# Projections and value products of two cross attentions put among the last batches, and normalised rows shared by VectorE and ScalarE

## The chip, the core and the metric

The program runs on one NeuronCore of a Trainium2 chip. The core has TensorE (PE: matmuls and transposes through an array of 128 x 128, with a separate load of the stationary operand, PEld), VectorE (DVE), ScalarE (ACT), GpSimd (POOL), and SyncE (SP), which only issues DMAs. Each engine works through its own queue in order and waits on semaphores for the others. Matmuls write to PSUM, eight banks of 512 float32 columns in 128 partitions. The metric is the device time of one execution in microseconds.

## What is computed

A Perceiver-like model of four layers on 32 sequences of 32 latent tokens with 256 features, in float32. Each layer has a cross attention to a context of 257 tokens a sequence, a self attention and a feed-forward part, most of them with mixtures of experts. The parts that the change touches most, cut down:

```python
# layer 1 cross attention (16 heads of 64, one key/value head), parallel feed-forward
h = layer_norm(x)                      # 1024 rows of 256
kv = layer_norm(context) @ Wkv
att = softmax(q(h) @ k.T) @ v          # by sequence
x = x + att @ Wo + (silu(gate) * up) @ Wff2
# layer 3 cross attention (8 heads of 64) over context and latents
x = x + (softmax(q @ keys.T) @ tokens) @ Wv @ Wout
# layer 0 experts
h = layer_norm(x); r = rms_norm(h); e = argmin(dist(r, centroids))
x = x + h + expert[e](r)
```

Every layer norm is a mean and a deviation by row, and then `(x - mean) / deviation`.

## The kernel before, in words

Twelve stages follow one another, one function each, with a barrier between them (`free_sems`, L87). X holds the 1024 rows as NT = 8 tiles of 128 rows. A stage normalises X into H, transposes H into HT and works on that.

**Norm** (L158). The last stage's end has already taken statistics tile by tile (`take`, L196: an addition to X, then L203 and L206 for its tiles). At the entry ScalarE takes the root (L235), VectorE the reciprocal (L213), and VectorE alone writes the eight normalised tiles one after the other (`rows`, L186), each with an increment of one semaphore. **Flip** (L238): TensorE transposes in the order half 0 chunk 0, half 0 chunk 1, half 1 chunk 0, half 1 chunk 1, four tiles each (L262), and waits before each for its tile. ScalarE copies the chunk 0 banks (L275, L279), VectorE the chunk 1 banks (L290, L294), which on VectorE is behind all eight rows. Eleven entries use this with a counter of rows; the twelfth, layer 0's experts, has a further norm (L2086).

**Layer 0's experts** (L2013). VectorE writes eight tiles of R (L2086), adds H to the whole of X in one instruction (L2088), and then makes its two copies of the transposed R (L290). TensorE's router (L1227, 16 products of 8 columns) needs these copies. From the router's result VectorE derives the places of all tokens (L2093 and on, `place_rows`, `place_weights`, `mark_columns`, `find_rows`, L756 to L841); GpSimd then gathers rows by indirect DMA (L997), and `ex.vector` begins with the first expert's units (L1168).

**Layer 1's cross attention** (L2110). After the query projection and the first feed-forward matrix, TensorE multiplies the second one tile by tile (L2293, banks 0 to 2 in turn) with keys and values of the first two batches in between; VectorE adds each tile to X (L2431). Then come 32 batches. In iteration b TensorE does `sim(b + 1)` (L2258, banks 0 to 3), `flip_probs(b)` (L2269, banks 4 and 5), `keys_values(b + 3)` (L2241, bank 6), `weigh(b)` (L2283, bank 7) and `flip_values(b + 3)` (L2247). ScalarE does the exponentials (L2342) and copies, `copy_out(b)` (L2355) writing 32 columns of AT; VectorE the maxima (L2410), reciprocals (L2415) and copies; GpSimd multiplies by the reciprocals (L2190). AT shares its memory with the hidden units of the feed-forward. The output projection (L2315) waits for all 32 batches, does 8 tiles of 8 matmuls with two tiles to a bank, and VectorE adds pairs of tiles to X and takes their statistics (L2456). Four filler matmuls (`keep_busy`, L81) end TensorE's part.

**Layer 3's cross attention** (L3300). 32 batches likewise, `flip_probs(b)` (L3409, L3412), `sim(b + 2)`, `weigh(b)` (L3425, L3428); the results replace QW. Behind the last one TensorE waits for ScalarE's copy (L3514) and makes 8 value products (L3459), for four pairs of heads by two halves of the sequences, alternately in banks 0 (copied by ScalarE, L3534) and 1 (by VectorE, L3592). When all are copied, the projection follows (L3466), added by pairs (L3596). The memory of OT is that of hat, tokens and probs of the batches.

## Time and profile before

| | |
|---|---|
| median of 3 runs | 1978.56 us (1977.77 to 1979.53) |
| profiled execution | 1979.34 us, span from first to last instruction 1977.6 us |
| TensorE matmul busy | 1811.5 us, 92% |
| VectorE busy | 1075.2 us, 54% |
| ScalarE busy | 808.4 us, 41% |
| GpSimd busy | 564.9 us, 29% |
| mean granted TensorE clock | 0.963 of 2.4 GHz |
| stage of layer 1's cross attention | 391.3 to 703.4 us |
| stage of layer 3's cross attention | 1520.2 to 1765.1 us |

Times within the trace count from the first instruction. A row of the timeline names an engine, a line of the kernel and an operation, and in brackets how long the engine had been idle before it and what ended that. A matmul in float32 leaves two records, and matmuls are pipelined, so their ends overlap; the weight loads show better when TensorE really went on. The granted clock is 1.00 at 2.4 GHz and 0.50 at 1.2 GHz.

### The profile page before, as it was taken

Reading aid. Unit: us, or ns where it says so; the run is one execution under the profiler, and the core shown is the slowest. Engines: PE = TensorE matmul, PEld = TensorE weight load, DVE = VectorE, ACT = ScalarE, POOL = GpSimd, SP = SyncE. Lnnn points to the kernel's source line nnn. Section 1 sums busy time; section 2 is a strip of 40 time slices with the busy share of each in tenths; the row PEclk is TensorE's granted clock in tenths of the full one; section 3 lists DMA queues with packets and bytes.
Section 4 is the critical chain, followed back from the end, with each engine's and each line's share of the span. In section 5 each row is a group of like instructions: output and inputs, shape, how many; then the busy total and the mean of one; then the engine's idle time right before and its main releaser. Section 6 shows DMA issues by size and latency. Waiting matters only on the chain. (4 is left out here: it accounts for less than half of the span.)

```text
span 1977.6 us, 43225 instructions
## 1 busy us (share of the span) xinstructions
PE 1811.5 (92%) x16810; PEld 1405.4 (71%) x16810; DVE 1075.2 (54%) x2695; ACT 808.4 (41%) x2340; POOL 564.9 (29%) x617
## 2 busy tenths in 40 slices
PE   8999779999999889799999989998588899987898
PEld 6886569844777756699999957776454477755787
DVE  7787841352366337875555545555665555437511
ACT  6663621122266334233333325553410566616232
POOL 4441313100144202311121113331311466515242
PEclk9999889999999999999999999998699999998899
DMA  4120068560233110041899641111011355300397
GB/s 146 55 56 5 3 239 296 192 217 30 57 102 100 28 54 3 8 195 58 310 330 334 225 169 50 50 45 54 2 54 57 89 157 155 102 1 2 109 338 253
DMA packets 87010, 233.92 MB, mean 118 GB/s; under 512 B 9776, under 2 KB 45136, under 8 KB 80304
## 3 DMA queue, kind: packets, MB, share of 16 engines
q1 hardware_dynamic: 78992, 213.90, 32.1%
q0 software_dynamic: 5664, 15.47, 2.5%
q8 instruction: 121, 1.98, 0.4%
q10 hardware_dynamic: 2176, 2.10, 0.3%
q14 instruction: 57, 0.47, 0.1%
HBM read 216.21 MB, written 12.07 MB: 115 GB/s over the span
## 5 line engine op out<-in xcount | busy, mean ns | idle before, releaser
L2190 POOL TENSOR_TENSOR l1x_probs<-l1x_probs,l1x_total 128x512 f32<-128x512 f32 x64 | 65.0, 1038 | 211.4 <-DVE l1x_total L2415 211.4
L1515 PE MATMUL PS<-weights,l0x_ctxT 128*128 128x256 f32 x512 | 121.0, 386 | 0.8 <-DVE l0x_kp L1803 0.7
L1048 PE MATMUL PS<-l1f_xT,l1f_slot 128*128 128x128 f32 x1024 | 117.0, 275 | 0.0
L1048 PEld LDWEIGHTS PS<-l1f_xT,l1f_slot 128*128 128x128 f32 x1024 | 115.7, 192 | 0.1
L1515 PEld LDWEIGHTS PS<-weights,l0x_ctxT 128*128 128x128 f32 x512 | 94.0, 190 | 15.9 <-issue 3.5
L2923 POOL TENSOR_TENSOR l2x_probs<-l2x_probs,l2x_total 128x512 f32<-128x512 f32 x64 | 65.1, 1038 | 136.3 <-DVE l2x_total L3097 136.3
L81 PE MATMUL PS<-consts 128*128 128x256 f32 x340 | 85.1, 403 | 17.5 <-PEq L87 15.8
L81 PEld LDWEIGHTS PS<-consts 128*128 128x128 f32 x340 | 67.5, 203 | 31.6 <-issue 19.5
L235 ACT ACTIVATE std<-moments,eps 128x8 f32<-128x8 f32 x13 | 3.9, 301 | 203.1 <-DVEq L173 133.7
L1175 DVE SCALAR_TENSOR_TENSOR l1f_product<-PS,l1f_slot,l1f_side 128x128 f32<-128x128 f32 x128 | 36.0, 344 | 65.9 <-ACT l1f_side L1131 50.9
L3401 PE MATMUL PS<-l3x_keysT,l3x_QW 128*128 128x289 f32 x256 | 67.7, 407 | 1.7 <-issue 1.7
L1002 POOL DMA_INDIRECT l1f_out_dram<-l1f_out,l1f_sort_target_row x23 | 22.6, 985 | 159.5 <-DVE l1f_out L1158 159.5
L1131 ACT ACTIVATE l1f_side<-PS,l1f_slot 128x128 f32<-128x128 f32 x128 | 36.5, 368 | 66.0 <-PE PS L1048 62.9
L3425 PE MATMUL PS<-tagged,l3x_QT 128*128 128x256 f32 x256 | 60.6, 379 | 1.9 <-ACT tagged L3510 1.9
L2950 PE MATMUL PS<-l2x_ctxT,weights 128*128 128x257 f32 x256 | 61.1, 381 | 1.0 <-DMA l2x_ctxT<-in_ctxT_dram 1.0
L1048 PE MATMUL PS<-HT,weights 128*128 128x128 f32 x512 | 60.7, 280 | 0.9 <-DVE l1f_gated L1180 0.7
L1048 PEld LDWEIGHTS PS<-HT,weights 128*128 128x128 f32 x512 | 60.1, 197 | 1.8 <-DVE l1f_gated L1180 1.1
L1695 ACT ACTIVATE l0x_sq<-PS 128x256 f32<-128x256 f32 x128 | 47.8, 385 | 32.6 <-PE PS L1515 32.6
L1175 DVE SCALAR_TENSOR_TENSOR l1f_product<-PS,weights,l1f_side 128x128 f32<-128x128 f32 x120 | 33.8, 344 | 49.7 <-ACT l1f_side L1131 41.0
L2958 PE MATMUL PS<-weights,l2x_ctxT 128*128 128x256 f32 x256 | 60.4, 379 | 0.0
L3043 ACT ACTIVATE l2x_probs<-PS,l2x_top 128x257 f32<-128x257 f32 x128 | 59.2, 482 | 1.3 <-DVE l2x_top L3091 1.3
L2232 PE MATMUL PS<-HT,weights 128*128 128x512 f32 x128 | 57.3, 608 | 2.2 <-DVE l1x_AT L2379 2.2
(659 smaller groups left out, 4648.5 us busy)
## 6 DMA issues: line engine op xcount, KB each, us to landing
l1f_slot<-in_experts_up_dram SPq DMA_DIRECT2D x16, 2056.0 KB
weights<-in_experts_up_dram SPq DMA_DIRECT2D x8, 2056.0 KB, 7.8
weights<-in_experts_down_dram SPq DMA_DIRECT2D x21, 640.0 KB, 4.3
weights<-in_experts_up_dram SPq DMA_DIRECT2D x10, 1024.0 KB
l1f_slot<-in_experts_down_dram SPq DMA_DIRECT2D x16, 640.0 KB, 4.1
l0x_ctxT<-in_ctxT_dram SPq DMA_DIRECT2D x32, 257.0 KB, 2.6
l1x_ctxT<-in_ctxT_dram SPq DMA_DIRECT2D x32, 257.0 KB
l2x_ctxT<-in_ctxT_dram SPq DMA_DIRECT2D x32, 257.0 KB, 2.6
```

Source lines behind the costliest of these rows:

```text
L81: self.nc.tensor.matmul(self.PS[:, bank, 0:2 * P], self.ident, self.consts[:, 0:2 * P], start=True, stop=True)
L1048: done = nc.tensor.matmul(PS[:, bank + a, m * P:(m + 1) * P], mat[:, c, m * P:(m + 1) * P], x, start=(c == 0), stop=(c == 1))
L1175: done = nc.vector.scalar_tensor_tensor(p[:, m, :], PS[:, 2 * u + 1, m * P:(m + 1) * P], w["b3"][:, 4 * u + m:4 * u + m + 1], self.side[u] ...
L1515: last = nc.tensor.matmul(PS[:, 2 * (b % 2) + k, half * D:(half + 1) * D], ctxT[b % SLOTS][:, c, half * P:(half + 1) * P], kw[:, c, k * D: ...
L2190: nc.gpsimd.tensor_tensor(p, p, bcast(total[b % 2][:, 2 * n:2 * n + 2], 2, KEYS), ALU.mult).then_inc(probs_done, 1)
L2232: done = nc.tensor.matmul(PS[:, 2 * (n % 2) + g, :], ff1[:, c, (g * HB + m) * P:(g * HB + m + 1) * P], core.HT[:, c, half * 512:(half + 1) ...
L2923: nc.gpsimd.tensor_tensor(p, p, bcast(total[b % 2][:, 2 * n:2 * n + 2], 2, 2 * P), ALU.mult).then_inc(probs_done, 1)
L2950: last = nc.tensor.matmul(PS[:, 4 + 2 * o, 0:CTX], wk[:, c, o * P:(o + 1) * P], ctxT[b % 2][:, c, :], start=(c == 0), stop=(c == 1))
L2958: last = nc.tensor.matmul(PS[:, 5, half * D:(half + 1) * D], ctxT[b % 2][:, c, half * P:(half + 1) * P], wv[:, c, :], start=(c == 0), stop ...
L3043: done = nc.scalar.activation(probs[b % 2][:, u, :], PS[:, u, 0:CTX], ACT.Exp, bias=top[b % 2][:, u:u + 1], scale=-1.0, accum_out=total[b ...
L3401: done = nc.tensor.matmul(PS[:, 2 * (b % 2) + u, 0:KEYS], QW[:, c, b, 4 * u:4 * u + 4, :].rearrange("p h q -> p (h q)"), keysT[b % 2][:, c ...
L3425: nc.tensor.matmul(PS[:, 6 + c, 0:2 * P], tokens[b % 2][:, half, c * P:(c + 1) * P], probsT[b % 2][:, half, :], start=(half == 0), stop=False)
```

## The change

1. **Norm rows.** At eleven entries VectorE first computes shift = -mean / deviation (one instruction for all tiles), then writes tiles 0, 2, 4, 6, 7; ScalarE, after the root, waits for the shift and writes tiles 1, 3, 5 as `scale * x + shift`. Two counters take the place of one, and all who waited (transposes, GpSimd, SyncE's stores of rows) wait for the two.
2. **Layer 0's experts.** The addition of H to X moves from before VectorE's copies to behind `find_rows`.
3. **Layer 1's cross attention.** Tile 7 of the feed-forward product (bank 7) goes behind `sim(0)`, its addition behind the first reciprocals; `weigh(0)` waits for it. Tile 0 of the projection goes before `weigh(30)`, tile 1 before `weigh(31)`; each tile waits for its own four batches. The last two tiles have banks of their own and are added one by one.
4. **Layer 3's cross attention.** The value products go by halves: products 0 to 3 for the first 16 sequences (all copied by ScalarE), 4 to 7 for the others (by VectorE); product 0 goes before the last `weigh`. The projection of the first four tiles waits for ScalarE's copies only. The last two tiles are added one by one.

The core of the diff; the same two-counter form and the call of `scalar_rows` come at all eleven entries:

```diff
+ROWS_BY_DVE, ROWS_BY_ACT = (0, 2, 4, 6, 7), (1, 3, 5)
...
+        self.shifts_dve += 1
+        nc.vector.scalar_tensor_tensor(c.shift[:], c.moments[:, :, 0], -1.0, c.rstd[:], ALU.mult, ALU.mult).then_inc(self.shift_done, 1)
+        for t in ROWS_BY_DVE:
             nc.vector.tensor_scalar(dst[:, t, :], src[:, t, :], c.moments[:, t, 0:1], c.rstd[:, t:t + 1],
-                                    ALU.subtract, ALU.mult).then_inc(rows_done, 1)
+                                    ALU.subtract, ALU.mult).then_inc(dve_done, 1)
+    def scalar_rows(self, act, src, dst, rows_done):
+        c, nc = self.core, self.core.nc
+        _, act_done = rows_done
+        self.shifts_act += 1
+        act.wait_ge(self.shift_done, self.shifts_act)
+        for t in ROWS_BY_ACT:
+            nc.scalar.activation(dst[:, t, :], src[:, t, :], ACT.Identity, bias=c.shift[:, t:t + 1], scale=c.rstd[:, t:t + 1]).then_inc(act_done, 1)
+    def wait_rows(self, eng, rows_done):
+        dve_done, act_done = rows_done
+        eng.wait_ge(dve_done, len(ROWS_BY_DVE))
+        eng.wait_ge(act_done, len(ROWS_BY_ACT))
     def statistics(self, dve):
...
+                    if isinstance(rows_done, tuple):
+                        if t in ROWS_BY_ACT:
+                            pe.wait_ge(rows_done[1], ROWS_BY_ACT.index(t) + 1)
+                        else:
+                            pe.wait_ge(rows_done[0], ROWS_BY_DVE.index(t) + 1)
+                    else:
+                        pe.wait_ge(rows_done, t + 1)
                     to, rows = c.PS[:, 2 * half + ch, (t % 4) * P:(t % 4 + 1) * P], src[:, t, ch * P:(ch + 1) * P]
...
+            norm.scalar_rows(act, core.X, core.H, rows_done)
...
-            dve_step(dve, nc.vector.tensor_tensor(core.X[:], core.X[:], core.H[:], ALU.add))
             flip.vector(dve, XT)
...
             ex.places.find_rows(dve)
+            dve_step(dve, nc.vector.tensor_tensor(core.X[:], core.X[:], core.H[:], ALU.add))
             ex.vector(dve)
...
+        def ff_bank(t):
+            return t % 3 if t < NT - 1 else 7
+        def out_bank(t):
+            return (6, 6, 5, 5, 4, 4, 1, 2)[t]
...
                     pe.wait_ge(out_copied, b)
+                else:
+                    pe.wait_ge(ff_added, NT)
...
             pe.wait_ge(less_v_done, 1)
-            for t in range(NT):
+            def feed_forward(t):
+                for m in range(HB):
+                    done = nc.tensor.matmul(PS[:, ff_bank(t), 0:D], hidden[:, m, t * P:(t + 1) * P], ff2[:, m, :], start=(m == 0), stop=(m == HB - 1))
+                done.then_inc(ff_done, 1)
+            def project(t):
+                pe.wait_ge(out_copied, TB * t + TB)
+                for m in range(HB):
+                    done = nc.tensor.matmul(PS[:, out_bank(t), (t % 2) * D:(t % 2 + 1) * D], AT[:, m, t * P:(t + 1) * P],
+                                            wo[:, m, :], start=(m == 0), stop=(m == HB - 1))
+                done.then_inc(out_done, 1)
+            for t in range(NT - 1):
                 if t >= 3:
                     pe.wait_ge(ff_added, t - 2)
-                for m in range(HB):
-                    done = nc.tensor.matmul(PS[:, t % 3, 0:D], hidden[:, m, t * P:(t + 1) * P], ff2[:, m, :], start=(m == 0), stop=(m == HB - 1))
-                done.then_inc(ff_done, 1)
+                feed_forward(t)
                 if t in (0, 4):
                     keys_values(t // 4)
                 elif t in (2, 6):
                     flip_values(t // 4)
-            pe.wait_ge(ff_added, NT)
+            pe.wait_ge(ff_added, NT - 1)
             sim(0)
+            feed_forward(NT - 1)
             keys_values(2)
             flip_values(2)
             for b in range(B):
...
                 flip_probs(b)
                 if b + 3 < B:
                     keys_values(b + 3)
+                if b == B - 2:
+                    pe.wait_ge(v_copied, B)
+                    project(0)
+                elif b == B - 1:
+                    project(1)
                 weigh(b)
                 if b + 3 < B:
                     flip_values(b + 3)
-            pe.wait_ge(out_copied, B)
-            for t in range(NT):
-                for m in range(HB):
-                    done = nc.tensor.matmul(PS[:, 4 + t // 2, (t % 2) * D:(t % 2 + 1) * D], AT[:, m, t * P:(t + 1) * P],
-                                            wo[:, m, :], start=(m == 0), stop=(m == HB - 1))
...
-                nc.vector.tensor_tensor(core.X[:, t, :], PS[:, t % 3, 0:D], core.X[:, t, :], ALU.add).then_inc(ff_added, 1)
+                nc.vector.tensor_tensor(core.X[:, t, :], PS[:, ff_bank(t), 0:D], core.X[:, t, :], ALU.add).then_inc(ff_added, 1)
+            def add_out(tiles):
+                first, n = tiles[0], len(tiles)
+                dve.wait_ge(out_done, tiles[-1] + 1)
+                x = core.X[:, first:first + n, :]
+                at = (first % 2) * D
+                written = nc.vector.tensor_tensor(x, PS[:, out_bank(first), at:at + n * D].rearrange("p (t d) -> p t d", t=n), x, ALU.add)
+                norm.take(dve, written, tiles)
+            for t in range(NT - 1):
+                add_feed_forward(t)
                 if t in (1, 5):
                     scale_keys_values(t // 4)
-                elif t in (3, 7):
+                elif t in (3, 6):
                     copy_values(t // 4)
             tops(0)
-            scale_keys_values(2)
             for n in range(2):
                 weights(0, n)
+            add_feed_forward(NT - 1)
+            scale_keys_values(2)
             copy_values(2)
             for b in range(B):
                 if b + 1 < B:
...
                     weights(b + 1, 1)
                 if b + 3 < B:
                     copy_values(b + 3)
-            for n in range(NT // 2):
-                dve.wait_ge(out_done, n + 1)
-                x = core.X[:, 2 * n:2 * n + 2, :]
-                written = nc.vector.tensor_tensor(x, PS[:, 4 + n, :].rearrange("p (t d) -> p t d", t=2), x, ALU.add)
-                norm.take(dve, written, (2 * n, 2 * n + 1))
+            for tiles in ((0, 1), (2, 3), (4, 5), (6,), (7,)):
+                add_out(tiles)
         cn.loads = B // cn.SLOTS
...
+        def out_bank(t):
+            return 4 + t // 2 if t < NT - 1 else 2
...
-            for b in range(B):
-                flip_probs(b)
-                if b + 2 < B:
-                    sim(b + 2)
-                weigh(b)
-            pe.wait_ge(px_copied, B)
-
-            for n in range(2 * M):
-                m, half = n // 2, n % 2
+            def values(n):
+                half, m = divmod(n, M)
+                pe.wait_ge(px_copied, (half + 1) * (B // 2))
                 if n >= 2:
-                    pe.wait_ge((out_act, out_dve)[n % 2], n // 2)
+                    pe.wait_ge(*((out_act, n - 1) if n - 2 < M else (out_dve, n - 1 - M)))
                 for par in range(2):
                     for c in range(C):
                         at = (2 * m + par) * DH
                         done = nc.tensor.matmul(PS[DH * par:DH * (par + 1), n % 2, :], wv[:, c, at:at + DH], QW[:, c, half * (B // 2):(half + 1) * (B // 2), 2 * m + par, :],
                                                 start=(c == 0), stop=(c == 1))
                 done.then_inc(out_done, 1)
-            pe.wait_ge(out_act, M)
-            pe.wait_ge(out_dve, M)
+            for b in range(B):
+                flip_probs(b)
+                if b + 2 < B:
+                    sim(b + 2)
+                if b == B - 1:
+                    values(0)
+                weigh(b)
+            for n in range(1, 2 * M):
+                values(n)
             for t in range(NT):
+                if t % 4 == 0:
+                    pe.wait_ge((out_act, out_dve)[t // 4], M)
                 for m in range(M):
-                    done = nc.tensor.matmul(PS[:, 4 + t // 2, (t % 2) * D:(t % 2 + 1) * D], OT[:, m, t * P:(t + 1) * P], wout[:, m, :],
+                    done = nc.tensor.matmul(PS[:, out_bank(t), (t % 2) * D:(t % 2 + 1) * D], OT[:, m, t * P:(t + 1) * P], wout[:, m, :],
                                             start=(m == 0), stop=(m == M - 1))
-                if t % 2:
-                    done.then_inc(proj_done, 1)
+                done.then_inc(proj_done, 1)
             core.keep_busy(0, 4)
...
                 copy_px(b)
-            for n in range(0, 2 * M, 2):
-                act.wait_ge(out_done, n + 1)
-                nc.scalar.activation(OT[:, n // 2, 0:512], PS[:, 0, :], ACT.Identity, bias=v_bias[:, n // 2:n // 2 + 1]).then_inc(out_act, 1)
+            for m in range(M):
+                act.wait_ge(out_done, m + 1)
+                nc.scalar.activation(OT[:, m, 0:512], PS[:, m % 2, :], ACT.Identity, bias=v_bias[:, m:m + 1]).then_inc(out_act, 1)
...
             dve.wait_ge(v_bias_copied, 1)
-            for n in range(1, 2 * M, 2):
-                dve.wait_ge(out_done, n + 1)
-                nc.vector.tensor_scalar(OT[:, n // 2, 512:1024], PS[:, 1, :], v_bias[:, n // 2:n // 2 + 1], None, ALU.add).then_inc(out_dve, 1)
-            for n in range(NT // 2):
-                dve.wait_ge(proj_done, n + 1)
-                x = core.X[:, 2 * n:2 * n + 2, :]
-                written = nc.vector.tensor_tensor(x, PS[:, 4 + n, :].rearrange("p (t d) -> p t d", t=2), x, ALU.add)
-                norm.take(dve, written, (2 * n, 2 * n + 1))
+            for m in range(M):
+                dve.wait_ge(out_done, M + m + 1)
+                nc.vector.tensor_scalar(OT[:, m, 512:1024], PS[:, m % 2, :], v_bias[:, m:m + 1], None, ALU.add).then_inc(out_dve, 1)
+            for tiles in ((0, 1), (2, 3), (4, 5), (6,), (7,)):
+                first, n = tiles[0], len(tiles)
+                dve.wait_ge(proj_done, tiles[-1] + 1)
+                x = core.X[:, first:first + n, :]
+                at = (first % 2) * D
+                written = nc.vector.tensor_tensor(x, PS[:, out_bank(first), at:at + n * D].rearrange("p (t d) -> p t d", t=n), x, ALU.add)
+                norm.take(dve, written, tiles)
         @block.gpsimd
```

## Rows read from the trace of the kernel before

**Rows 1.** Timeline (start, busy us), weight loads, last batches of layer 1.
```profile
666.63 0.88 PEld L2283 LDWEIGHTS PS<-l1x_probsT,l1x_V 128*64 128x64 f32 x16 [1.20 <-issue]
668.43 0.42 PEld L2269 LDWEIGHTS PS<-consts,l1x_probs 128*128 128x128 f32 x4 [0.92 <-issue]
669.37 0.42 PEld L2269 LDWEIGHTS PS<-consts,l1x_probs 128*128 128x128 f32 x4 [0.52 <-POOL l1x_probs L2190]
671.07 0.88 PEld L2283 LDWEIGHTS PS<-l1x_probsT,l1x_V 128*64 128x64 f32 x16 [1.28 <-issue]
672.75 1.38 PEld L2315 LDWEIGHTS PS<-weights,l1x_AT 128*128 128x128 f32 x7 [0.81 <-ACT l1x_AT L2355]
```

**Rows 2.** One line, layer 1's projection: ns min/median/max, first to last start.
```profile
L2315 PE MATMUL PS<-weights,l1x_AT x128: 379/379/483, 672.8 to 700.3; 128*128 128x256 f32 x128
```

**Rows 3.** Timeline, all engines, from layer 1's feed-forward into its batches.
```profile
521.63 0.18 PEld L2258 LDWEIGHTS PS<-l1x_kvT,l1x_QT 64*128 64x128 f32 x1 [0.92 <-DVE X L2431]
522.70 0.73 PEld L2241 LDWEIGHTS PS<-l1x_ctxT,l1x_centred_kv 128*128 128x128 f32 x4 [0.33 <-issue]
526.42 0.17 DVE L2415 RECIPROCAL l1x_total<-l1x_total 128x2 f32<-128x2 f32 x1 [0.75 <-ACT l1x_probs L2342]
526.50 0.18 PEld L2258 LDWEIGHTS PS<-l1x_kvT,l1x_QT 64*128 64x128 f32 x1 [1.94 <-issue]
```

**Rows 4.** Timeline, weight loads, end of layer 3's cross attention.
```profile
1730.09 1.59 PEld L3425 LDWEIGHTS PS<-tagged,l3x_QT 128*128 128x128 f32 x8 [1.14 <-ACT tagged L3506]
1733.40 0.20 PEld L3459 LDWEIGHTS PS<-l3x_QW,weights 128*64 128x64 f32 x4 [1.09 <-ACT l3x_QW L3514]
1748.31 0.73 PEld L3466 LDWEIGHTS PS<-weights,l3x_QT 128*128 128x128 f32 x4 [1.79 <-issue]
```

**Rows 5.** One line, the value products of layer 3.
```profile
L3459 PE MATMUL PS<-l3x_QW,weights x64: 592/592/643, 1733.4 to 1746.8; 128*64 128x512 f32 x64
```

**Rows 6.** Timeline, ends of layer 1's cross attention and of layer 2's experts.
```profile
700.49 1.89 PE L81 MATMUL PS<-consts 128*128 128x256 f32 x8
700.69 0.69 DVE L2456 TENSOR_TENSOR X<-PS,X 128x512 f32<-128x512 f32 x1 [5.15 <-PE PS L2315]
702.20 0.25 DVE L206 BATCH_NORM_AGGREGATE moments<-stats 128x2 f32<-128x6 f32 x2
703.37 0.34 SPq L126 DMA_DIRECT2D weights<-in_pack_dram  x1
...
1520.26 1.10 PE L81 MATMUL PS<-consts 128*128 128x256 f32 x4 [0.70 <-PEq L87]
```

**Rows 7.** Timeline, entry of layer 1's experts.
```profile
838.85 2.71 DVE L186 TENSOR_SCALAR tagged<-X,moments,rstd 128x256 f32<-128x256 f32 x8
841.61 0.53 PEld L262 LDWEIGHTS PS<-consts,tagged 128*128 128x128 f32 x5 [0.18 <-DVE tagged L186]
```

**Rows 8.** One line, ScalarE, 128x256 with bias and scale, layer 3.
```profile
L3488 ACT ACTIVATE l3x_QT<-l3x_ctx,ctx_shift,ctx_rstd x64: 587/600/626, 1562.8 to 1720.8; 128x256 f32<-128x256 f32 x64
```

**Rows 9.** Timeline, entry of layer 2's cross attention.
```profile
1156.71 2.50 PEld L262 LDWEIGHTS PS<-consts,tagged 128*128 128x128 f32 x13 [0.19 <-DVE tagged L186]
```

**Rows 10.** Timeline, layer 0's experts, up to the first expert.
```profile
260.91 2.28 DVE L2088 TENSOR_TENSOR X<-X,tagged 128x2048 f32<-128x2048 f32 x1
264.07 5.19 PE L1227 MATMUL PS<-l0f_centm,l0f_XT 128*128 128x8 f32 x32 [1.91 <-DVE l0f_XT L290]
283.09 1.20 POOL L997 DMA_INDIRECT l0f_rows_in<-l0f_rows_dram,l0f_sort_token_row  x1 [26.83 <-DVE l0f_sort_token_row L836]
298.94 0.69 DVE L1168 TENSOR_TENSOR l0f_hidden<-PS,l0f_side 128x512 f32<-128x512 f32 x1 [16.10 <-ACT l0f_side L1119]
```

**Rows 11.** Windows: length, PE PEld DVE ACT POOL busy, clock, DMA, GB/s.
```profile
264.00:266.00 2.00, 1.93 (x18) 1.96 (x18) 0.52 (x1) 1.20 (x7) 0.00 (x0) 1.00 1.24 378
266.00:269.40 3.40, 3.26 (x16) 3.16 (x16) 0.03 (x1) 0.00 (x0) 0.00 (x0) 0.50 0.56 193
...
842.30:846.00 3.70, 3.70 (x34) 3.70 (x34) 0.69 (x1) 1.55 (x2) 3.47 (x4) 1.00 0.94 318
```

98 lines of the change are left out of this document (64 added, 34 removed).

## The prediction

> **What bounds the kernel now.** I read three views in this order. First the page: TensorE is busy for 92% of the span, so what can still be won lies in the gaps between its instructions, not in less work; the change removes no matmul. Then, for each place that the diff touches, the timeline in narrow stretches, TensorE's weight loads above all: a load that starts late with a releaser in brackets is a gap, and its size stands there. Last the windows with the granted clock, for the places where a gap is followed by slow matmuls. The change goes at five kinds of them: the end of layer 1's batch loop [rows 1, 2], the step from its feed-forward into the batches [rows 3], the end of layer 3's loop [rows 4, 5], the last additions of both stages [rows 6], and in front of transposes the entries of stages [rows 7 to 9] and the router of layer 0's experts, which waits for a large addition [rows 10, 11].
>
> **Layer 1, last batches.** Before weigh(30), both halves of flip_probs(31), weigh(31) and the first projection matmul the loads sit idle for 1.20, 0.92, 0.52, 1.28 and 0.81 us: 4.73 in all [rows 1]. The projection is 64 matmuls, 128 records, the first at 672.8, the last at 700.3 [rows 2]: 0.215 us a record, 3.44 us a tile of 16. The change puts tile 0 before weigh(30) and tile 1 before weigh(31), and each later tile waits for its own four batches only, so all but tile 7 are free to go. Both inserts (3.44) are longer than the gaps that they fill (1.20, 1.28), and while they run the next inputs arrive: by the times of before GpSimd's shares for batch 31 land at 669.3 [rows 1], and flips(30) (ends 1.20 before 666.63, 665.4) plus tile 0 (3.44) plus weigh(30) (0.88) is 669.7. What is queued behind weigh(30) is ScalarE's copy_out(30) and then copy_probs(31); it comes after flips(31), which are later too, so it is no new wait. What is left of the five gaps is pipeline drain. Bounds: 4.73, and 3.9, if each junction keeps a drain of 0.16 (a record takes 0.379, the next starts 0.215 after it [rows 2]). I take 4.3, the middle.
>
> **Layer 1, feed-forward.** Before sim(0) the loads are idle 0.92, before sim(1) 1.94 [rows 3]. Now tile 7 (3.44) goes between sim(0) and keys_values(2). Call S the start of sim(0). Before, sim(1) is at S + 4.87. After, S comes 3.44 + 0.05 earlier (it waits for the addition of tile 6, about as near as that of tile 7 was), sim(0) takes 1.07, tile 7 3.44, and keys_values(2) to sim(1) goes as before without the 1.94: 526.50 - 1.94 - 522.70 = 1.86 [rows 3]. That is S - 3.49 + 6.37 = S + 2.88, 2.0 earlier. The exponentials, at S + 4.79 by the second reciprocal [rows 3], are done before S + 6.37, and VectorE's addition of tile 7 fits between that reciprocal and scale_keys_values(2), 1.4 us. weigh(0) gets a new wait for that addition, which by then is over a microsecond old. The batch loop behind has its own pace and starts 2.0 earlier.
>
> **Layer 3.** The gaps of the loads are 1.14 (before the last weigh), 1.09 (before the value products) and 1.79 (before the projection): 4.02 [rows 4]. Value product 0 goes into the first, products 1 to 3 no longer wait for the last copy, and the projection of the first four tiles needs ScalarE's copies only, which are long done. A product's records have 512 columns and run on after their loads: the last starts at 1746.8 and takes 0.592 [rows 5], so that only 0.9 of the last gap is empty for certain. Bounds 4.02, and 2.7 (0.98 and 0.93 after a drain of 0.16 each, less 0.1, and 0.9). I take 3.0, nearer the low one.
>
> **The single last tiles.** At the end of layer 1's cross attention VectorE's last pair goes from its addition (0.69, at 700.69) to the end of its aggregates at 702.45, and the next stage starts at 703.37 [rows 6]. With one tile these 1.76 are about 1.1 (half of each instruction, some fixed part kept). But TensorE's four filler matmuls end at 702.38, and where they held the barrier (into layer 3's cross attention) the next stage's first matmul came 0.70 after them, its first other instruction a little sooner [rows 6]. So the next stage can't start before 703.05: 0.3 gained, not 0.65. Bounds 0 and 0.6. Twice: 0.65.
>
> **Normalised rows on two engines.** Eleven norms change. At the entry of layer 1's experts eight rows on VectorE take 2.71 us, 0.33 apart; the last reaches TensorE at 841.61, and five transposes (0.53) follow [rows 7]. After: a small shift instruction goes ahead (some 0.08 of VectorE's time) and VectorE has five rows, so its last is there at about 840.7. ScalarE's three cost 0.60 each by the nearest row, the same form with two per-partition operands (I space them 0.50 apart, as VectorE's 0.41 are 0.33 apart) [rows 8]: ready at 839.65, 840.15, 840.65. Row 3 then comes no earlier than before (840.24), and from it on 13 transposes at 0.11 are the bound: 841.67 against 842.14. Gain 0.47, also for the router, which follows at once. That holds where transposes run at the upper clock level: layer 0 self, layer 1 self and experts, layer 3 self (first norm) and experts, five times: 2.35. In the other six the transposes take 0.2 each and form an unbroken row (13 loads in 2.50) [rows 9]; rows are not late there, and the shift and ScalarE's slower first row can cost some 0.05 each: -0.3. In layer 1 cross they wait for another matmul anyway. Together 2.05; from -1 (ScalarE's rows late by as much as they are now early) to 3.4 (0.65 five times).
>
> **Layer 0 experts.** X + H is 2.28 us in front of VectorE's two copies, and the router waits 1.91 for them, to 264.07 [rows 10]. It moves behind find_rows, where VectorE is idle for 16.1 us until 298.94 [rows 10]: cost nothing under that cover, 2.28 without it. The first copy then goes where the addition went, at 260.91, and the router starts where TensorE is free, at 264.07 - 1.91 = 262.16: 1.9 gained. The second part is clock. The router's first 18 matmuls ran at granted 1.00 (2.4 GHz), the next 16 at 0.50 (1.2 GHz) [rows 11]; before them TensorE had been nearly idle for 1.9 us. In layer 1 the router has no such gap and all 34 are at 1.00 [rows 11]; the fall comes behind it. So I expect 3.5 us instead of 5.19, 1.55 more: 3.45 together. What follows (sorting, gathers) hangs on the router by a chain and moves with it.
> The moved addition overlaps GpSimd's first gathers; the first takes 1.20 at 283.09 [rows 10], with small VectorE instructions beside it. The Trainium skill, SBUF — State Buffer, section Who interferes with whom, says that a VectorE instruction with two SBUF inputs takes a port pair from GpSimd and that the later of the two fully blocks; it infers, without showing, that descriptor generation is spared. By the blocking rule the sum would come to up to 1965.4, by the inference to 1963.1. No row here has such an overlap; I take 0, since the gather's 1.20 beside short VectorE instructions is no sign of a full block, and keep 2.28 as the other bound.
>
> **Sum.** 4.3 + 2.0 + 3.0 + 0.65 + 2.05 + 3.45 = 15.45. The profiled execution has a span of 1977.6 (1979.34 with what lies around it); the median of the three runs is 1978.56, 0.8 below that execution. 1978.56 - 15.45 = **1963.1**.
>
> **Rivals.**
> (a) ScalarE's rows win nothing, since row 3 or 5 comes later than reckoned: the 2.35 go, 1965.5. For: 0.60 a row against 0.41. Against: five rows of VectorE end 0.9 earlier whatever ScalarE does.
> (b) Layer 0's experts win little: the moved addition holds the gathers (2.28), or the clock falls in the router all the same (1.55). 1964.7 to 1965.4. The first is a port that GpSimd would have to wait for, its price the addition's length; the second has for it that the fall in layer 1 came right behind the router.
> (c) The inserts shift the last batches' waits instead of filling them, so that half of layer 1's and layer 3's ends stays: 3.65 less, 1966.8. Against: every input of the inserted work is four or more batches old.
> (d) It doesn't do what it says: what is won in a stage is lost in front of the next, on weights or a barrier. Only some 3 us remain, 1975.5. Against: stage entries wait for the barrier alone (released by L87, the barrier) [rows 6].
> (e) Slower: TensorE's clock falls in the packed projections. All 128 records of layer 1's are within 379 to 483 ns now [rows 2]; at the lower level they double. If its 27.5 us all run so, 1963.1 + 27.5 = 1990.6. It decides from 19.5 us of matmuls at 1.2 GHz on (15.5 to cancel the gain, 4 to be slower). Against: gaps are filled, and in the rows clocks fall behind gaps or narrow matmuls.
>
> **How the numbers follow.** Chances: forecast 0.57, (a) 0.12, (b) 0.14, (c) 0.09, (d) 0.04, (e) 0.04. All low bounds together give 3.9 + 2.0 + 2.7 + 0 - 1 - 0.4 = 7.2 (1971.4); all high ones 4.73 + 2.0 + 4.02 + 1.2 + 3.4 + 3.45 = 18.8 (1959.8). The range takes (a), (b), (c) and two of them at once: 1959.3 to 1969. 0.2% is 4.0 us, about what a measurement of this kernel can tell from no change: faster is the forecast with (a) to (c), 0.92; same is (d), 0.04; slower (e), 0.04.
>
> **What would show it.** In the profile after: loads of the projection at once behind flips(30) and flips(31); no gap over 0.4 us between weigh(31) and the end of the projection; sim(1) 2.0 earlier relative to the feed-forward; in layer 3 no gap between products and projection; the last row-bound transposes 0.5 earlier after the reciprocal; the router of layer 0 in about 3.5 us, 1.9 earlier; the first gather still at 1.2. I am wrong if the stage of layer 1 cross (391.3 to 703.4) shortens by less than 5 us or that of layer 3 (1520.2 to 1765.1) by less than 2.5, or if the gathers take 3 us.

## The result and the profile after

The changed kernel takes 1959.75 us in the median of eight runs (1957.67 to 1971.24), the kernel before 1978.56 in eight beside it (1973.59 to 1982.61): a ratio of 0.9916, 95% interval 0.9899 to 0.9933. Run once more later, without a line changed, it gave 1963.8 (0.9921, 0.9897 to 0.9945); all fourteen runs together have the median 1962.3. Forecast were 1963.1. The profiled execution spans 1957.4 us, the one before 1977.6.

The page of after: TensorE is busy for 1800.9 us, 10.6 less than before, although no matmul is gone, so part of the gain is the same work at a higher clock (mean granted 0.967, before 0.963).

```profile
span 1957.4 us, 43250 instructions
PE 1800.9 (92%) x16810; PEld 1399.4 (71%) x16810; DVE 1066.5 (54%) x2675; ACT 826.2 (42%) x2373; POOL 567.1 (29%) x617
PEclk9999889999999999999999989999699999997899
```

**Layer 1, last batches.** Timeline of the weight loads (start, busy us, then engine, line, operation; in brackets the idle time before and what ended it).

```profile
657.16 3.32 PEld L2341 LDWEIGHTS PS<-weights,l1x_AT 128*128 128x128 f32 x16
660.81 0.85 PEld L2327 LDWEIGHTS PS<-l1x_probsT,l1x_V 128*64 128x64 f32 x16 [0.33 <-issue]
661.84 0.86 PEld L2311 LDWEIGHTS PS<-consts,l1x_probs 128*128 128x128 f32 x8 [0.17 <-issue]
...
666.32 0.85 PEld L2327 LDWEIGHTS PS<-l1x_probsT,l1x_V 128*64 128x64 f32 x16 [0.33 <-issue]
667.34 8.71 PEld L2341 LDWEIGHTS PS<-weights,l1x_AT 128*128 128x128 f32 x41 [0.17 <-issue]
```

The five gaps of [rows 1], 4.73 us, are 0.33, 0.17, none, 0.33 and 0.17 now, which I read as the drain between one group of matmuls and the next. From the first load of sim(29) to the first filler it is 45.88 us before and 41.78 after; 4.10 won.

```profile
654.39 0.18 PEld L2258 LDWEIGHTS PS<-l1x_kvT,l1x_QT 64*128 64x128 f32 x1 [0.17 <-issue]
700.27 1.70 PEld L81 LDWEIGHTS PS<-consts 128*128 128x128 f32 x8
```

```profile
646.17 0.18 PEld L2300 LDWEIGHTS PS<-l1x_kvT,l1x_QT 64*128 64x128 f32 x1 [0.17 <-issue]
687.95 1.70 PEld L83 LDWEIGHTS PS<-consts 128*128 128x128 f32 x8
```

**Layer 1, feed-forward.** The same view of after. Sim(0) starts 10.01 earlier than in [rows 3]. The first tile of the feed-forward already starts 6.34 earlier (484.70, before 491.04), so 3.67 are tile 7 and what was waited for; sim(1) comes 6.54 behind it instead of 4.87, and is 8.34 earlier: 2.00 won.

```profile
511.62 0.18 PEld L2300 LDWEIGHTS PS<-l1x_kvT,l1x_QT 64*128 64x128 f32 x1 [0.54 <-DVE X L2487]
512.69 3.32 PEld L2335 LDWEIGHTS PS<-weights,l1x_AT 128*128 128x128 f32 x16 [0.33 <-issue]
518.16 0.18 PEld L2300 LDWEIGHTS PS<-l1x_kvT,l1x_QT 64*128 64x128 f32 x1 [0.17 <-issue]
```

**Layer 3.** The gaps of [rows 4] were 1.14, 1.09 and 1.79; they are 0.81, 0.33 and 0.81.

```profile
1713.42 1.59 PEld L3504 LDWEIGHTS PS<-tagged,l3x_QT 128*128 128x128 f32 x8 [0.81 <-issue]
1715.98 0.20 PEld L3533 LDWEIGHTS PS<-l3x_QW,weights 128*64 128x64 f32 x4 [0.33 <-issue]
1728.20 1.81 PEld L3550 LDWEIGHTS PS<-weights,l3x_QT 128*128 128x128 f32 x9 [0.81 <-issue]
```

**The single last tiles.** All engines at the end of layer 1's cross attention. VectorE is done at 689.47, the fillers at 690.05, and the next stage's first matmul comes 0.96 after them, where one row of [rows 6] had made me expect 0.70. From the first filler load to the next stage's root on ScalarE it was 3.20 us before, and is 3.12: 0.08 won.

```profile
688.16 1.89 PE L83 MATMUL PS<-consts 128*128 128x256 f32 x8
688.37 0.42 DVE L2494 TENSOR_TENSOR X<-PS,X 128x256 f32<-128x256 f32 x1 [2.35 <-PE PS L2341]
689.29 0.18 DVE L230 BATCH_NORM_AGGREGATE moments<-stats 128x2 f32<-128x6 f32 x1
691.01 1.10 PE L83 MATMUL PS<-consts 128*128 128x256 f32 x4 [0.96 <-PEq L89]
691.07 0.30 ACT L259 ACTIVATE std<-moments,eps 128x8 f32<-128x8 f32 x1 [21.62 <-DVEq L176]
```

**Rows by two engines**, the entry of layer 1's experts. From VectorE's first instruction behind the reciprocal to the end of the transposes it is 2.86 us (824.51 to 827.37), before 3.29 (838.85 to 842.14 [rows 7]): 0.43 won. ScalarE's three rows take 1.59 together, 0.50 apart, and end with VectorE's five, at 826.4.

```profile
824.51 0.28 DVE L195 SCALAR_TENSOR_TENSOR shift<-moments,rstd 128x8 f32<-128x8 f32 x1
824.72 1.73 DVE L197 TENSOR_SCALAR tagged<-X,moments,rstd 128x256 f32<-128x256 f32 x5
824.83 1.59 ACT L206 ACTIVATE tagged<-X,shift,rstd 128x256 f32<-128x256 f32 x3 [0.59 <-DVE shift L195]
825.97 1.40 PEld L292 LDWEIGHTS PS<-consts,tagged 128*128 128x128 f32 x13 [0.29 <-ACT tagged L206]
```

**Layer 0's experts.** The router starts at once behind the matmuls ahead of it and its 32 loads take 3.65 us, all at 2.4 GHz. But the first gather takes 3.14 where [rows 10] had 1.20. It starts 0.22 after the moved addition and ends 1.07 after that has ended; the gathered rows are transposed 8.74 after it began, before 6.04.

```profile
261.56 3.65 PEld L1261 LDWEIGHTS PS<-l0f_centm,l0f_XT 128*128 128x128 f32 x32
278.91 2.29 DVE L2141 TENSOR_TENSOR X<-X,tagged 128x2048 f32<-128x2048 f32 x1
279.13 3.14 POOL L1031 DMA_INDIRECT l0f_rows_in<-l0f_rows_dram,l0f_sort_token_row  x1 [23.29 <-DVE l0f_sort_token_row L866]
287.87 0.29 PEld L1062 LDWEIGHTS PS<-consts,l0f_rows_in 128*128 128x128 f32 x2 [6.89 <-DMA l0f_rows_in<-l0f_rows_dram,l0f_sort_token_row]
```

Added up by places, these make less than the 20.2 us between the two spans. The rest lies where the diff changes nothing. Windows of after, then of before (length, busy of PE, PEld, DVE, ACT, POOL, granted clock, DMA, GB/s): the entry of layer 1's cross attention, where TensorE ran at 1.2 GHz for 4 us after, and before from 392 to 403.

```profile
388.00:392.00 4.00, 3.81 (x15) 3.19 (x16) 2.06 (x7) 2.06 (x5) 1.44 (x3) 0.57 0.59 174
392.00:396.00 4.00, 3.00 (x15) 1.87 (x15) 3.51 (x9) 1.38 (x2) 0.00 (x0) 1.00 0.30 102
```

```profile
392.00:396.00 4.00, 3.38 (x16) 3.01 (x16) 2.67 (x8) 0.78 (x1) 0.89 (x2) 0.54 0.80 263
396.00:403.00 7.00, 6.00 (x14) 3.28 (x13) 5.21 (x13) 1.35 (x2) 0.00 (x0) 0.53 0.29 88
```

By the table of stage lengths below, that stage is 3.0 us longer with 6.8 us of low time than with 3.4. Five more such stretches (at 737, 894, 1375, 1453 and 1771 before) are gone after, while one is new (1163 to 1171). Is that the change's doing or chance? And do the parts add up to the whole?

### The profile page after: what moved, and what is told of

Its sections match the earlier page's. It is cut to its first block and busy times, and to the rows that moved or that the text cites. A ratio compares the mean times of both kernels' runs of the same rounds, so it can differ in the third digit from the quotient of the medians.

```text
span 1957.4 us, 43250 instructions
## 1 busy us (share of the span) xinstructions
PE 1800.9 (92%) x16810; PEld 1399.4 (71%) x16810; DVE 1066.5 (54%) x2675; ACT 826.2 (42%) x2373; POOL 567.1 (29%) x617
```

## Experiments

Twelve more programs ran, two of them the kernels before and after once more. Theory A says that the low stretches of the clock fall where chance puts them, theory B that the change removes them, theory L that the addition holds the gather.

### Each part alone

`only_rows`, `only_l1x`, `only_l3x` and `only_move` are the kernel before with one part of the diff each. The last three also carry the second counter of the norm rows, but it stays unused: VectorE writes all eight rows, as before. Beyond that, the last one is only this:

```diff
-            dve_step(dve, nc.vector.tensor_tensor(core.X[:], core.X[:], core.H[:], ALU.add))
             flip.vector(dve, XT)
...
             ex.places.find_rows(dve)
+            dve_step(dve, nc.vector.tensor_tensor(core.X[:], core.X[:], core.H[:], ALU.add))
             ex.vector(dve)
```

> The kernel before with one part of the change alone: the normalised rows of eleven norms by VectorE (five) and ScalarE (three). The change as a whole won 18.8 us by the medians, but by a comparison of the two traces only some 13 of them (4.1 + 2.0 + 3.4 in the cross attentions, 3.5 in layer 0's experts) stand where the prediction put them; five short stretches in which the clock was at 1.2 GHz before (737 to 741, 894 to 898, 1375 to 1379, 1453 to 1458, 1771 to 1775) are gone, and one is new. Theory A (the clock's stretches move by accident when anything is shifted): this kernel gains its 2 us of rows (0.4 to 0.6 at each of five entries), and a clock sum that may go either way by up to 5: 1971 to 1979, with another set of low stretches than either kernel. Theory B (the denser transposes are what keeps the clock up at the entries): the stretches behind entries of layer 2 self, layer 2 experts and the second norm of layer 3 self are gone here as in the whole change, and the gain is 5 us or more.

> The kernel before with layer 1's cross attention changed alone (feed-forward tile 7 behind the first sim, projection tiles 0 and 1 among the last batches, single last tiles). Both theories: inside that stage the trace shows 2.0 us won by the first two sims, 4.1 to 4.3 at the last batches and 0.2 to 0.3 at the last tiles, 6.4 together. Theory A: the low stretches behind it (737 to 741, 894 to 898, entries of layers 2 and 3) are then another set than before, so the time is 1972 with an accident of up to 5 either way. Theory B: they stay where they were, since no transposes change: 1972, within 1.

> The kernel before with layer 3's cross attention changed alone. Both theories: nothing before 1730 us differs from before, and from there to the next stage's first instruction 3.0 to 3.4 us are won, 0.75 of it between the last weigh and the value products and 2.7 before the projection. Time 1975. Behind it theory A allows other low stretches in layer 3's self attention and experts (up to 2 either way); theory B none. It tells also how steady the pattern of low stretches ahead of the edit is between two executions: nothing there differs, so whatever moves there is the chip's.

> The kernel before with the addition of layer 0's experts moved behind the search for rows, alone. In the trace of the whole change the first gather took 3.14 us instead of 1.20 while the addition (2.29) ran, and the first gathered rows were transposed 8.7 us after that gather began, not 6.0. Theory L (the addition holds the gather, the prediction's rival b, its first half): the first gather takes 3.1 here too, starts 3.9 earlier than before, and of these 3.9 about 3.2 reach the first expert's matmuls. Theory D (the delay is the weights' transfers, which come earlier too): gather 1.2 to 1.5 here. The router's 34 matmuls start 1.9 earlier and take 3.6 in either. Time 1975 (theory L), with accidents of the clock up to 5 either way if theory A holds.

Measured in twelve runs each, beside 35 of before with the median 1978.28: rows 1977.14 (ratio 0.9990, 0.9978 to 1.0003), layer 1 1970.02 (0.9962, 0.9951 to 0.9973), layer 3 1977.26 (0.9999, 0.9987 to 1.0011), moved addition 1977.22 (0.9996, 0.9984 to 1.0008). The gains 1.1, 8.3, 1.0 and 1.1 make 11.5; the whole has 16 to 17. The traces are sharper than the times. The last batches of layer 1 win 4.09 in `only_l1x`, as in the whole. The last tiles win 0.08 there, where I had expected 0.2 to 0.3. `only_l3x` wins 2.54 in its stage, not 3.0 or more. In `only_move` the gather behaves as in the whole, which is what theory L says:

```profile
279.71 2.29 DVE L2129 TENSOR_TENSOR X<-X,tagged 128x2048 f32<-128x2048 f32 x1
279.92 3.15 POOL L1019 DMA_INDIRECT l0f_rows_in<-l0f_rows_dram,l0f_sort_token_row  x1 [24.05 <-DVE l0f_sort_token_row L855]
```

The gather began 3.17 us earlier than before, not 3.9, since the router's loads took 4.26 us here and not 3.6. Of that, 1.75 reached VectorE's first product of the first expert (297.19, before 298.94), not 3.2.

And `only_l3x`, which does the same as before for 1700 us, has a low stretch at 185 to 190 where the kernel before has none (first its window, then that of before):

```profile
185.00:190.00 5.00, 4.03 (x18) 3.14 (x17) 3.70 (x10) 1.17 (x2) 0.00 (x0) 0.66 0.10 31
```

```profile
185.00:190.00 5.00, 4.12 (x19) 2.44 (x20) 3.35 (x9) 1.17 (x2) 0.00 (x0) 1.00 0.06 22
```

It lost 1.0 us there. For theory B `only_rows` should have lost its low stretches at three entries; it has one at each (1370 to 1374, 1448 to 1453, 1766 to 1773). Theory B falls for the rows.

### Both kernels once more

`again` is the changed kernel, `before_again` the kernel before, no line different.

> The changed kernel once more, not a line different. Theory A (the low clock stretches fall where chance puts them): its trace has another set of stretches at 1.2 GHz than the first trace of the same kernel, and of the five that had vanished there at least two are back; its span is longer by what they cost. The stage-internal gains (2.0, 4.1, 3.4, 0.5 at an entry) stand as they were. Theory B (the change itself removes them): the same stretches as in the first trace, within one. On the time: the four parts alone sum to 11 to 12 us by their medians, the whole came out 16.6 to 18.8 better on eight runs, three of which were at 1968 to 1971. If parts and whole agree, this gives 1962 to 1967; if the parts help each other, 1959 to 1961.

> The kernel before once more, for a second trace of it: between two executions of the same code the stages without a low clock stretch keep their lengths within 0.1 us, and the stretches at 1.2 GHz differ in place or length in at least three spots (theory A). By theory B they are the same as in the first trace. The low stretch at the entry of layer 3's self attention (1771 to 1775) is there again, if it belongs to the gaps ahead of it.

`again`: 1963.8 in six runs, span 1961.8; up to 450 its low stretches are those of the first trace but for one that is gone (241 to 249), then it has new ones at 774 to 778 and 1439 to 1444. Of the five vanished one is back, not two as theory A had it here. The wins inside the stages stand (2.00 and 4.10 in layer 1, 2.54 in layer 3). `before_again`: 1978.7, span 1977.0; none any more at 242 to 249, 737 to 741 or 894 to 898, but one at 283 to 287 and one in the first batches of layer 1. Its window from 525 to 529, then that of the first trace of the same code:

```profile
525.00:529.00 4.00, 4.00 (x24) 3.16 (x26) 2.19 (x6) 2.42 (x9) 1.26 (x3) 0.57 0.10 21
```

```profile
525.00:529.00 4.00, 2.47 (x19) 2.12 (x20) 2.08 (x6) 1.88 (x9) 2.03 (x2) 1.00 0.47 115
```

From sim(0) to sim(2) it then needs 10.87 us instead of 9.45: a clock accident of 1.4 us in the middle of what I had costed. The low stretch at the entry of layer 3's self attention is there again (1768 to 1771). So the stretches move between two executions of one kernel, as theory A says, although much of a pattern repeats.

### The addition behind the gathers

`add_between` lets VectorE wait until three gathers are issued; a one-column memset on GpSimd gives the signal.

```diff
         for i in range(RING):
             gather(i)
+        nc.gpsimd.memset(mark[:], 0.0).then_inc(issued, 1)
...
+            dve.wait_ge(issued, 1)
             dve_step(dve, nc.vector.tensor_tensor(core.X[:], core.X[:], core.H[:], ALU.add))
```

> The changed kernel with one more wait: VectorE's addition of layer 0's experts starts only when GpSimd has issued its first three gathers (a one-column memset behind them gives the signal). Theory L (the addition held the first gather): the first gather takes 1.2, the three are issued within 3.7 us, the addition runs behind them, and the first gathered rows are transposed about 6.0 us after the first gather began, not 8.7; 0.8 us reach the experts for certain (the router's 3.95 instead of 3.18), up to 2.7 if the weights are there. Theory D (weights or the transfers set it): gather times change but the first transposes stay 8 us behind. Time 0.8 below the changed kernel, inside the scatter.

```profile
280.30 1.20 POOL L1031 DMA_INDIRECT l0f_rows_in<-l0f_rows_dram,l0f_sort_token_row  x1 [23.45 <-DVE l0f_sort_token_row L866]
284.21 2.29 DVE L2146 TENSOR_TENSOR X<-X,tagged 128x2048 f32<-128x2048 f32 x1 [4.17 <-POOL l0f_mark L1044]
286.39 0.20 PEld L1065 LDWEIGHTS PS<-consts,l0f_rows_in 128*128 128x128 f32 x2 [4.25 <-DMA l0f_rows_in<-l0f_rows_dram,l0f_sort_token_row]
```

The gather is back at 1.20 and the transposes 6.09 behind its start. Over all traces it is never otherwise: the six in which addition and gather overlap have 3.14 or 3.15 and first transposes 8.6 to 8.9 behind; the eight in which they don't have 1.20, and 5.9 to 6.1. Theory L is shown. Of the 2.65 us at the transposes some 1.1 (standard error 0.3) reach the stage's length (below). The time, 1965.1 in four runs (0.9919, 0.9899 to 0.9940), can't tell that.

### A third insert, and the fillers

```diff
-            return (6, 6, 5, 5, 4, 4, 1, 2)[t]
+            return (6, 6, 3, 3, 5, 5, 1, 2)[t]
...
-                if b == B - 2:
-                    pe.wait_ge(v_copied, B)
-                    project(0)
-                elif b == B - 1:
-                    project(1)
+                if b == B - 3:
+                    pe.wait_ge(v_copied, B)
+                if b >= B - 3:
+                    project(b - (B - 3))
```

> The changed kernel with three projection tiles among layer 1's last batches, not two: tile 0 before weigh(29), 1 before weigh(30), 2 before weigh(31), tiles 2 and 3 in a score bank that is free by then. The loads stood idle for 1.20 before weigh(29) and 0.52 before sim(31). If an insert fills whatever gap it meets (the prediction's mechanism), the idle before weigh(29) falls to 0.33 and that before sim(31) to 0.2, and the projection ends 1.0 to 1.2 earlier relative to sim(29). If the rival holds (inserts only shift the waits of the last batches), the end of the projection does not move.

From sim(29) to the first filler it is 40.35 us, in the changed kernel 41.78: 1.43 more won, since the gap of 1.20 before weigh(29) is down to 0.33 too, and that of 0.52 before sim(31) to 0.17:

```profile
654.63 3.32 PEld L2341 LDWEIGHTS PS<-weights,l1x_AT 128*128 128x128 f32 x16
658.29 0.85 PEld L2327 LDWEIGHTS PS<-l1x_probsT,l1x_V 128*64 128x64 f32 x16 [0.33 <-issue]
```

An insert fills the gap that it meets; the rival, that the waits only shift, is out here. Time 1963.6 in four runs (0.9919, 0.9900 to 0.9938).

`no_fillers` leaves out the filler matmuls (they compute nothing that is used) at the ends of layers 1's and 3's cross attention:

```diff
-            core.keep_busy(0, 4)
```

> The changed kernel without TensorE's four filler matmuls at the end of layers 1's and 3's cross attention. The single last tiles won less than forecast: the next stage's first instruction came 3.23 after the fillers' first load before, 3.15 now, 0.08 won and not 0.33, and VectorE's last aggregate ends 0.58 before the last filler. If the fillers hold the barrier, the next stage starts 0.5 to 0.6 earlier here, at each of the two ends, 1.1 together. If the barrier goes by VectorE or another queue, nothing moves. The rival price: TensorE is idle for 3 us instead of 1 ahead of the transposes, and they run at the lower clock level, 1.7 lost for each entry.

ScalarE's root comes 2.13 after VectorE's last addition (689.63 to 691.76), not 2.70: the fillers did hold the barrier, for 0.57. And the price is there as well. The window shows the clock, the timeline 13 loads in 2.64 us where 1.40 were enough:

```profile
693.00:697.00 4.00, 3.66 (x16) 2.91 (x16) 2.05 (x6) 2.30 (x5) 0.00 (x0) 0.57 0.99 354
```

```profile
691.67 0.73 PEld L83 LDWEIGHTS PS<-consts 128*128 128x128 f32 x4 [2.48 <-issue]
693.68 2.64 PEld L292 LDWEIGHTS PS<-consts,tagged 128*128 128x128 f32 x13 [0.29 <-ACT tagged L206]
```

No other of the fourteen traces has a low stretch at that entry. But this is one trace, and low stretches move between executions, so that the missing fillers caused it is likely and not shown. Time 1967.5 (0.9933, 0.9913 to 0.9953), the slowest with the whole change. The price is not paid at every entry: at layer 3's self attention the transposes kept 2.4 GHz.

### Layer 3 taken out of the whole

> The changed kernel with layer 3's cross attention as before. That part alone on the kernel before gave a ratio of 0.9999 (0.9987 to 1.0011), though its trace shows 3.45 us won between the last batch and the last filler. If the gain is real in the end, this kernel is 3.4 slower than the whole change: 1965.5. If it is given back behind the stage (by the experts' weights in layer 3, which must arrive), it is within 1 of it. Every kernel with that stage changed has no low clock stretch at the entry of layer 3's self attention (five of five), every one without has one (five of five): if the filled gaps keep the clock up there, this kernel has it back, at 1746 to 1753, and loses another 1 to 2 us: 1966.5.

`no_l3x` has 1962.9 in five runs (0.9911, 0.9890 to 0.9933): by the times the part is worth 0.6, alone 0.2 to 1.0. Its trace says otherwise. From the first load of the last batch's weigh but one to the first filler it is 36.27 us here, as in the kernel before (1725.75 to 1762.02), and 33.72 with the new stage (1708.18 to 1741.90 in after, the same length in `add_between`): 2.55 won, less than the 3.4 that the expectation gave it. The two stages behind it last 212.4 us on average in the six traces with the old one and 212.3 in the eight with the new, so no giving back is seen; single traces run from 209.5 to 216.1, so these means can hide one of about 1 us. The 2.6 us are shown inside the stage. That they reach the kernel's time is not shown by the medians, nor excluded: the interval of `only_l3x` ends at 2.6 us. My own finding of the moment, that filled gaps keep the clock up behind that stage, is wrong: `no_l3x` has the gaps, and no low stretch at the entry.

### What beats both

`best` is the third insert with the later addition, `best_two_fillers` has two fillers instead of four at both ends besides.

> The changed kernel with the third insert in layer 1's last batches and the addition of layer 0's experts behind the first three gathers together. The traces of the two alone show 1.4 us won at the end of the projection and 0.6 at the end of the first expert. If they add, and nothing but chance moves the clock's stretches: 2.0 us below the changed kernel, 1960 to 1962 against the 1962 of its fourteen runs together. If it is within 0.5 of the changed kernel, the wins of a stage are given back behind it.

> The kernel with the third insert and the later addition, and two filler matmuls instead of four at the ends of layers 1's and 3's cross attention. Without any filler the next stage started 2.13 after VectorE's last addition, not 2.70, so the fillers held the barrier for 0.57; but all 13 transposes behind it then ran at 1.2 GHz (2.64 instead of 1.40). Two fillers end 0.94 before the four did, so VectorE is the last again and the 0.57 are won at both ends, 1.1 together; TensorE is idle for 0.4 longer than with four, not 2. If idle time is what lets the clock fall there, these entries keep 2.4 GHz and the kernel is 1 us below the one with four: 1959. If they are at 1.2 GHz again, it is even or up to 1.5 above.

1960.2 (0.9904, 0.9884 to 0.9925) and 1959.3 (0.9896, 0.9877 to 0.9915), each in five runs. Against the 1962.3 of the changed kernel that is 2.1 and 3.0 better, as added up, though the intervals overlap, so that either is better is not shown by the times. Two fillers win the 0.57 (next stage 2.13 after the last addition) and, at layer 1's self attention, the clock stays up:

```profile
687.35 0.43 DVE L2498 TENSOR_TENSOR X<-PS,X 128x256 f32<-128x256 f32 x1 [2.35 <-PE PS L2346]
689.48 0.30 ACT L259 ACTIVATE std<-moments,eps 128x8 f32<-128x8 f32 x1 [17.60 <-DVEq L176]
691.40 1.40 PEld L292 LDWEIGHTS PS<-consts,tagged 128*128 128x128 f32 x13 [0.29 <-ACT tagged L206]
```

At the other end with two fillers it fell. In layer 3's self attention the transposes of the first norm still ran at 2.4 GHz, but from 1754.7 to 1761.5 the clock was at 1.2, and the 13 transposes of the second norm took 2.47 us, in the changed kernel 1.40:

```profile
1754.47 2.47 PEld L292 LDWEIGHTS PS<-consts,l3a_QK 128*128 128x128 f32 x13 [0.29 <-ACT l3a_QK L206]
```

None of the seven other traces with the new layer 3 has a low stretch there, and the two stages from there on last 216.1 us, the longest of all. `no_fillers` has none there either, so this is no proof against two fillers; it is one trace, as is the one for them.

### Stage lengths and the clock

To part the change from the clock: the length of a stage, from root to root of its first norm, and in brackets its low time, the sum of 1 minus the granted clock over it, in us. It is what would be lost if the matmuls alone set the pace.

| kernel | l0 experts | l1 cross | l1 self | l1 experts | l3 cross | all low |
|---|---|---|---|---|---|---|
| before | 138.6 (8.5) | 312.0 (6.8) | 134.8 (1.7) | 316.4 (3.4) | 241.5 (1.7) | 72.4 |
| before_again | 138.8 (10.2) | 310.2 (5.1) | 133.4 (0.0) | 314.4 (1.7) | 241.6 (1.7) | 73.9 |
| only_rows | 140.5 (11.9) | 309.1 (3.4) | 134.2 (3.4) | 312.8 (0.2) | 241.4 (1.7) | 75.1 |
| only_l1x | 140.5 (11.9) | 305.9 (6.8) | 134.7 (1.7) | 314.0 (1.7) | 241.6 (1.7) | 78.8 |
| only_move | 137.4 (8.5) | 309.1 (3.4) | 134.9 (1.7) | 316.3 (3.4) | 241.3 (1.7) | 73.8 |
| only_l3x | 138.7 (8.5) | 309.0 (3.4) | 134.9 (1.7) | 316.2 (3.4) | 238.8 (1.7) | 71.7 |
| after | 135.9 (6.8) | 302.8 (3.4) | 132.9 (0.0) | 314.2 (1.7) | 238.8 (2.6) | 64.9 |
| again | 136.2 (6.8) | 302.9 (3.4) | 133.4 (1.7) | 314.0 (1.7) | 238.8 (1.7) | 64.9 |
| add_between | 135.4 (6.8) | 302.7 (3.4) | 134.3 (1.7) | 315.7 (3.8) | 240.9 (5.1) | 71.8 |
| three_inserts | 137.4 (10.4) | 301.2 (3.3) | 134.3 (1.7) | 314.1 (1.7) | 238.7 (1.7) | 68.3 |
| best | 136.8 (10.2) | 301.3 (3.4) | 134.2 (3.4) | 312.8 (0.2) | 238.7 (1.7) | 72.2 |
| no_fillers | 135.9 (6.8) | 302.2 (3.4) | 134.3 (1.7) | 315.6 (3.4) | 240.3 (5.1) | 78.5 |
| no_l3x | 140.5 (13.7) | 303.1 (3.4) | 133.3 (1.7) | 314.3 (1.7) | 243.1 (4.8) | 73.4 |
| best_two_fillers | 136.7 (10.2) | 300.6 (3.4) | 133.0 (0.0) | 315.8 (3.4) | 238.1 (1.7) | 74.3 |

Lengths at the same low time compare like with like: layer 1's cross attention 309.0 to 309.1 without its part, 302.7 to 303.1 with it and four fillers; layer 3's 241.3 to 241.6 against 238.7 to 238.8. A least-squares fit of each stage over the 14 traces (constant, slope on the low time, one effect for each part present) gives for layer 1's cross attention 6.1 won (standard error 0.1) and 1.6 more by the third insert, for layer 3's 2.8 (0.1), for layer 0's experts 1.4 (0.3) and 1.1 (0.3) more by the later addition, and for the eight other stages with normalised rows 1.9 together (0.9). Fewer fillers are worth 0.7 (0.1) and 0.5 (0.2) in the two cross attentions, which agrees with the 0.57 of the rows. The four parts of the change make 12.2, beside 11.5 from the parts' medians.

The whole has 16.7 by medians, and 15.4 by means (fourteen runs at 1963.7, all 80 of before at 1979.1). The eight traces with the change in it (`no_l3x` among them) have 3.3 less low time on average than the six others; at the fitted slopes, 0.3 to 0.9 a us, that is some 2 us, an estimate. The remaining 1 to 2.5 lie within the errors. Whether the change makes low stretches rarer or these executions had luck stays open: the two sets overlap (64.9 to 78.5 against 71.7 to 78.8).

## Why the prediction was right, and where not

The forecast of 1963.1 lies 0.8 above the median of fourteen runs, but 3.3 above that of the first eight, which is only 0.5 inside the lower end of the range. The mechanisms were mostly right. That the number fits is partly luck: the terms as measured below make 12.1, not 15.45, and two of them were too large by 2.6 together. What made up for it is a gain of the whole beyond its parts, some 2 us of it less low time, which no term had and which no run shows to be the change's doing. Of the signs that the prediction named for itself two came out against it: the first gather took 3.14, and in layer 3 a gap of 0.81 is left between products and projection.

- **Layer 1, last batches:** 4.3 forecast, 4.10 measured, between the bounds. Nothing new waits. Rival (c) is out.
- **Layer 1, feed-forward:** 2.0 forecast, 2.00 measured. Sim(1) is at S + 6.54, I had 6.37; S came 3.67 earlier, I had 3.49.
- **Layer 3:** 3.0 forecast, 2.55 measured, a little under the low bound 2.7. By the weight loads the insert won 0.82 before the last weigh (0.98 reckoned), the next gap 0.75 (0.83), and the projection 0.97 (0.9). The term that I mis-sized is the first: 0.81 of idle is left there, behind a product whose records of 592 ns [rows 5] outlast their loads; that these are the cause I only read from the lengths.
- **Single last tiles:** 0.65 forecast, 0.15 measured (0.08 and 0.07). The step that failed is the barrier's floor: I took 0.70 between filler and next stage from one row of [rows 6], of another stage; here it is 0.96 to 0.98. The same group held a better figure: before, at this very place, the next stage's first instruction comes 0.92 after VectorE's last aggregate (702.45 to 703.37). The mechanism, fillers as the new bound, is right: without them, or with two, 0.57 more is there.
- **Rows on two engines:** 2.05 forecast, 1.9 (error 0.9) by the fit, 0.43 at the entry that I had costed at 0.47. ScalarE's rows were 0.50 apart, as taken. Rival (a) is out there; stage by stage the fit is too coarse. (The high bound of 3.4 is given as five times 0.65, which is 3.25; only the sum of all high bounds uses it.)
- **Layer 0's experts:** 3.45 forecast, 1.4 at equal low time. The 1.9 of the router's wait is gone in all nine traces with the move. Two steps failed. First "cost nothing under that cover": I looked for VectorE's idle time, and it was there, but GpSimd was not free beside it. The value lay in my range, and the reason in rival (b); I chose the wrong end on a misread row. I took the gather's 1.20 at 283.09 for one beside short VectorE instructions, but the same [rows 10] have VectorE idle for the 16.10 us before 298.94, so from 282.84 on: the gather ran alone, and its 1.20 said nothing for or against a block. Second, the clock: I had it fall because of the 1.9 us gap ahead of the router. Without the gap the router's loads took 3.65 in four traces, and 4.26, 5.42, 5.45, 5.46 and 6.95 us in the others, with it 4.85 to 6.90: the clock fell between 261 and 268 in every trace, gap or none. Both halves of rival (b) are true in part.
- **Rival (d)**, lost in front of the next stage: no; **(e)**, the clock in the packed projections: no; none of the fourteen traces has a low stretch in the projection of layer 1 or of layer 3.

On the addition the rows show a gather that starts 0.22 after a VectorE instruction with two SBUF inputs and ends 1.07 after its end. Alone it takes 1.20, so it made next to no progress meanwhile. The Trainium skill, SBUF — State Buffer, Who interferes with whom, says that such an instruction contends with a GpSimd instruction that reads SBUF and that of two contenders the later one fully blocks; these runs agree (3.14 against 1.20). Its inference that descriptor generation is spared by such an instruction is not borne out for this gather, and the measurement decides. The gather also reads its indices from SBUF, and whether that read or the descriptors are held up no run here tells.

## What to carry to other kernels

Work whose inputs are some batches old fills the gaps at a loop's end down to some 0.3 us or less; count the gaps that are still there (a third insert was worth 1.4 us more). Before you move an instruction into an engine's idle time, look at what the other engines start in that moment: a large two-input VectorE instruction belongs behind GpSimd's gathers. And when TensorE's clock changes level on its own, compare stages at equal low time in several traces of the same kernel before an effect of 2 us is put down to an edit. At a barrier four fillers held the next stage up by 0.57, two did not. What the fillers do for the clock is open: it fell behind one of two ends without them, and in the stage behind one of two ends with two.

## What the runs showed of the hardware that I had not expected

An indirect gather took 3.14 to 3.15 us instead of 1.20, six times of six, while a 128x2048 addition of 2.29 us ran on VectorE. TensorE's granted clock went to 1.2 GHz at other places in two executions of one kernel, on one core, and the sum of low time ranged from 65 to 79 us; single runs of the changed kernel lie between 1957.4 and 1973.0, the 80 of before between 1973.2 and 1986.4.
